# Four graph layers on one core: the weight products of three layers as seven half-size products

## The reference

```python
# L0: x1 = x @ W1 + b1 (512 wide); four times g = g + gcn(g), gate alpha = tanh(p[dst] + q[src] + gb) per edge
#     out = concat([x1, g])
# L1: two sage layers
h   = relu(x @ W_self0 + mean(x)[neighbours] @ W_neigh0 + b0)
out =      h @ W_self1 + mean(h)[neighbours] @ W_neigh1 + b1
# L2: attention
h = x @ W;  e = exp(-leaky_relu(al[src] + ar[dst], 0.1))
out = elu(segment_sum(e * h[dst], src) / (rowsum + 1e-5))
# L3: gcn with loops
out = relu(D^-1/2 (A + I) D^-1/2 (x @ W) + b)
```

## Time and profile before

| | |
|---|---|
| median of 3 runs | 1536.47 us (1536.3 to 1537.12) |
| profiled execution, span from the first to the last instruction | 1534.3 us |
| its own time outside the span | not shown |
| TensorE busy | 1515.2 us, 6985 matmuls |
| VectorE, ScalarE, GpSimd busy | 883.6, 753.9, 187.2 us |
| moved by DMA | 231.75 MB, mean 151 GB/s |
| granted TensorE clock | 0.998 |

### The profile page before, as it was taken

One profiled execution on the slowest core, in us unless ns is written; L12 is line 12 of the kernel. 1 busy time (PEld: TensorE's weight loads), 2 busy tenths in 40 slices (PEclk: granted clock), 3 DMA queues, 4 the chain that ended last, 5 costly groups with the idle time before them and its releaser, 6 DMA issues.

```text
span 1534.3 us, 19219 instructions
## 1 busy us (share of the span) xinstructions
PE 1515.2 (99%) x6985; PEld 1220.1 (80%) x6985; DVE 883.6 (58%) x1410; ACT 753.9 (49%) x1348; POOL 187.2 (12%) x307
## 2 busy tenths in 40 slices
PE   7999999999999999999999999999999999999997
PEld 6887877878887887788878777888888778877776
DVE  9888788887545442423332353567598356436346
ACT  7677767768633342433332233345696246533233
POOL 0110021333200000000000000212053013100003
PEclk9999999999999999999999999999999999999999
DMA  6333154226764424333354424554466248545336
GB/s 200 123 122 107 47 191 132 84 78 224 261 237 149 161 96 155 119 113 116 114 171 130 143 81 166 196 203 166 147 197 190 94 143 297 182 131 171 94 121 186
DMA packets 103198, 231.75 MB, mean 151 GB/s; under 512 B 23162, under 2 KB 25972, under 8 KB 103096
## 3 DMA queue, kind: packets, MB, share of 16 engines
q1 hardware_dynamic: 90126, 191.62, 39.3%
q10 hardware_dynamic: 12970, 38.77, 6.6%
HBM read 170.98 MB, written 59.37 MB: 150 GB/s over the span
## 4 chain that ended last, share of the span: by engine, by line
PE 96%; DVE 3%; ACT 1%; issue 0%; DMA 0%; POOLq 0%; DVEq 0%; ACTq 0%
PE bank L986 18%; PE bank L842 16%; PE bank L844 15%; PE bank L843 15%; PE bank L997 9%; PE bank L990 9%; PE bank L988 9%; PE bank L1075 2%; PE bank L912 2%; PE bank L880 1%; DVE oK L1801 0%; ACT Tt L1159 0%; DVE wl L1445 0%; DVE Tt L1483 0%; DVE oL L1791 0%
## 5 line engine op out<-in xcount | busy, mean ns | idle before, releaser
L842 PE MATMUL bank<-wh,xh 128*125 128x512 f32 x1032 | 413.4, 401 | 0.9 <-ACT xh L1124 0.9
L843 PE MATMUL bank<-wl,xh 128*125 128x512 f32 x1040 | 410.3, 395 | 0.0
L844 PE MATMUL bank<-wh,xl 128*125 128x512 f32 x1040 | 409.6, 394 | 0.0
L986 PE MATMUL bank<-Zh,Mh 125*125 125x512 f32 x990 | 394.9, 399 | 0.0
L1457 DVE TENSOR_TENSOR xl<-xs,xh 128x1000 fp32r<-128x1000 f32 x130 | 155.5, 1199 | 291.0 <-ACT xh L1124 290.6
L1124 ACT CAST xh<-xs 128x1000 fp32r<-128x1000 f32 x130 | 132.9, 1026 | 303.0 <-PE bank L844 290.8
L997 PE MATMUL bank<-Zl,Mh 125*125 125x512 f32 x590 | 232.5, 394 | 0.0
L844 PEld LDWEIGHTS bank<-wh,xl 128*125 128x125 f32 x1040 | 193.0, 186 | 48.9
L843 PEld LDWEIGHTS bank<-wl,xh 128*125 128x125 f32 x1040 | 193.1, 186 | 45.4
L842 PEld LDWEIGHTS bank<-wh,xh 128*125 128x125 f32 x1032 | 191.0, 185 | 46.6 <-ACT xh L1124 1.1
L986 PEld LDWEIGHTS bank<-Zh,Mh 125*125 125x125 f32 x990 | 183.5, 185 | 44.0
(11 more groups left out here) (188 smaller groups left out, 1825.3 us busy)
## 6 DMA issues: line engine op xcount, KB each, us to landing
xs<-xT_d SPq DMA_DIRECT2D x80, 500.0 KB, 3.6
Ar<-a_d SPq DMA_DIRECT2D x100, 312.5 KB, 3.4
xs<-hT_d SPq DMA_DIRECT2D x40, 500.0 KB, 3.4
x_d<-XO ACTq DMA_DIRECT2D x30, 512.0 KB, 4.7
R<-x_d SPq DMA_DIRECT2D x60, 256.0 KB, 4.2
xT_d<-XT ACTq DMA_DIRECT2D x30, 500.0 KB, 3.8
ws<-in_W SPq DMA_DIRECT2D x30, 256.0 KB, 3.6
Tt<-m_d SPq DMA_DIRECT2D x10, 625.0 KB, 4.5
```

The lines of the kernel that those rows point to most:

```text
L842: te.matmul(o, xh[i % 2][:, k, :], wh[s][:], start=(k == 0), stop=False)
L843: te.matmul(o, xh[i % 2][:, k, :], wl[s][:], start=False, stop=False)
L844: m = te.matmul(o, xl[i % 2][:, k, :], wh[s][:], start=False, stop=(k == 7))
L986: te.matmul(o, Mh[i][:, s, :], zh, start=(n == 0), stop=False)
```

## The change

```diff
+ORDER = (("sw", 0), ("sw", 1), ("ag", 0), ("sw", 2), ("sw", 3), ("ag", 1), ("sw", 4), ("ag", 2), ("sw", 5), ("ag", 3))
+    for kind, n in ORDER:
+        if kind == "sw":
+            jobs += [Job("sw", w=n, p=p, t=t) for p in range(NP) for t in range(NH)]
+        else:
+            jobs += [Job("ag", d, a=n, f=f) for d in range(NT) for f in (1, 0)]
...
+            def weight_product(j):
...
+                for k in range(4):
+                    q.wait_ge(s_sh, 4 * P + k + 1)
+                    q.wait_ge(s_sl, 4 * P + k + 1)
+                    a, b = uh[U_RING[u]][:, k * T:(k + 1) * T], ul[U_RING[u]][:, k * T:(k + 1) * T]
+                    te.matmul(o, a, SH[h][k][:], start=(new and k == 0), stop=False, skip_group_check=not new)
+                    te.matmul(o, a, SL[h][k][:], start=False, stop=False, skip_group_check=not new)
+                    m = te.matmul(o, b, SH[h][k][:], start=False, stop=(k == 3), skip_group_check=not new)
```

```diff
+    UNIT_AT.setdefault(max(_j - 3, _late - 1), []).append(_u)
+    UNIT_LOAD.setdefault(max(_j - 5, _late - 2), []).append(_u)
...
+            def load_unit(u):
...
+                if u >= 3:
+                    q.wait_ge(s_ul, u - 2)
...
+                sy.dma_start(us[U_RING[u]][:], src).then_inc(d_us[U_RING[u]], 16)
...
+            def unit_lower(u):
+                q.wait_ge(s_uh, u + 1)
+                ve.tensor_tensor(ul[U_RING[u]][:], us[U_RING[u]][:], uh[U_RING[u]][:].bitcast(f32), ALU.subtract).then_inc(s_ul, 1)
```

```diff
+            def weight_sums(m, which):
+
+                b = TB[m // 4 in (1, 2, 3, 4)]
+                q.wait_ge(d_tb, 32 * (m + 1))
+                for i in which:
+                    o, x, y = ((0, 1, 0), (1, 3, 1), (3, 3, 0), (2, 2, 3))[i]
+                    if i:
+                        q.wait_ge(s_tsum, 4 * m + i)
+                    po.tensor_tensor(b[:, o, :], b[:, x, :], b[:, y, :], ALU.subtract).then_inc(s_tsum, 1)
```

```diff
+            def node_sums(n):
...
+                q.wait_ge(s_te, TE[X_GROUP[I, NH + t]])
+                q.wait_ge(d_x1[S_X[n]], 16 * sum_uses(S_X, S_X[n], n))
...
+                chain("v", ve.tensor_tensor(o[:, QW:2 * QW], x5[:, 0:QW], x5[:, QW:2 * QW], ALU.add))
+                chain("v", ve.tensor_tensor(o[:, 0:QW], a[:, 0:QW], x5[:, 0:QW], ALU.subtract))
+                mine()
+                chain("v", ve.tensor_tensor(a[:, 0:QW], o[:, QW:2 * QW], a[:, 0:QW], ALU.subtract))
+                mine()
+                ve.tensor_tensor(a[:, QW:2 * QW], a[:, QW:2 * QW], a[:, 0:QW], ALU.subtract).then_inc(s_sum4, 1)
```

```diff
+            for j in range(NT - 1, NJ + 2):
...
+                    store_own(j - 1)
+                for n in S_STORE.get(j, []):
+                    store_s(n)
+                for m in SUM_STORE.get(j, []):
+                    store_sum(m)
+                for i in PAIR_LOAD.get(j, []):
+                    load_pair(i)
+                for u in UNIT_LOAD.get(j, []):
+                    load_unit(u)
```

More of the change, by code:

```diff
@@ L94, with micros, before @@
 NJ = len(JOBS)
[L97 to L133, removed]
 J0 = {k: next(j for j, job in enumerate(JOBS) if job.kind == "gate" and job.layer == k) for k in range(4)}
 LAST_GATE = J0[3] + NT - 1
+SJ = [[[next(j for j, o in enumerate(JOBS) if o.kind == "sw" and (o.w, o.p, o.t) == (w, p, t)) for t in range(NH)]
+       for p in range(NP)] for w in range(6)]
+AJ = [[[next(j for j, o in enumerate(JOBS) if o.kind == "ag" and (o.a, o.d, o.f) == (a, d, f)) for f in range(2)]
+       for d in range(NT)] for a in range(4)]
+YI = {j: i for i, j in enumerate(j for j, job in enumerate(JOBS) if job.kind == "ag")}
+def micros(job):
+    if job.kind == "x1":
+        return 5.6
+    if job.kind == "gate" or (job.kind == "ag" and job.a == 2):
+        return 6.95
+    return 2.78 if job.kind == "sw" else 4.63
+START = [0.0] + list(accumulate(micros(job) for job in JOBS))
+def before(j, us):
+    return max(k for k in range(j) if START[k + 1] <= START[j] - us)
 LAST_ORDER = (8, 9) + tuple(range(8))
@@ L280, in r_uses, with att_mul, tile_done @@
-def r_uses():
-    of, by, n = {}, {}, 0
-    for j, job in enumerate(JOBS):
-        many = (0, 2, 1, 1)[job.layer] if job.kind == "gate" else \
-            1 if (job.layer == 2 and job.second) or job.kind in ("att", "kept", "loop") or j in W2_AT else 0
-        of[j] = list(range(n, n + many))
-        for i in of[j]:
-            by[i] = j
-        n += many
-    return of, by
-R_OF, R_BY = r_uses()
+    return MCUM[j - NT]
+def att_mul(d):
+    return ECUM[-1] + d + 1
+def tile_done(a, d):
+    return MCUM[-1] + NT * a + d + 1
@@ new lines, in r_uses @@
+def r_uses():
+    uses, of = [], {}
+    for j, job in enumerate(JOBS):
+        if job.kind == "gate":
+            what = [("gate", j)] * (0, 2, 1, 1)[job.layer]
+        elif job.kind == "sw" and (job.p == 1 or (job.p == 4 and job.w in SELF)):
+            what = [("store" if job.w in SELF else "z", j)]
+        elif job.kind == "ag":
+            what = [("ag", j)] * (1 + (job.a == 1))
+        else:
+            what = []
+        of[j] = list(range(len(uses), len(uses) + len(what)))
+        uses += what
+    return uses, of
@@ L367, with bank_of @@
-WC_GROUPS = [i for j in range(NJ) for i, w, _ in GROUPS[j] if w == "wc"]
-STORE = {j: i for i, j in enumerate(STORES)}
+@dataclass
+class Group:
+    what: str
+    bank: int
+    d: int = 0
+    n: int = 0
+    job: int = 0
+def bank_of(j):
+    job = JOBS[j]
+    if job.kind == "x1":
+        return 4 + j % 2
+    if job.kind == "gate":
+        return (j - NT) % 6
+    if job.kind == "sw":
+        return 5 + job.t % 2 if job.p == 1 else (job.t + 1) % 5
+    return (5, 0, 1, 2, 3, 4)[YI[j] % 20 % 6]
@@ new lines, with row_group @@
+GROUPS, GROUPS_BEFORE, GROUPS_AFTER, PREV = places()
+TE = list(accumulate(g.what != "sum" for g in GROUPS))
+X_GROUP = {(g.job, g.d): i for i, g in enumerate(GROUPS) if g.what == "x" and g.n == 1}
+ATT_GROUP = {g.d: i for i, g in enumerate(GROUPS) if g.what == "att"}
+WC_LAST = max(i for i, g in enumerate(GROUPS) if g.what == "wc")
+def row_group(k, d):
+    if k:
+        return next(i for i, g in enumerate(GROUPS) if g.what == "row" and g.job == J0[k - 1] + row_pair(d).stop - 1)
+    return ROW_GROUP if d < 4 else next(i for i, g in enumerate(GROUPS) if g.what == "rows" and d in ROWS[g.n])
@@ L750, in late @@
                         store_left(d - 1)
-                elif job.kind == "gate" and job.layer == 2:
+                elif job.layer == 2:
                     if d == 0:
```

2295 lines of the change are left out of this document (1309 added, 986 removed).

## The result

The changed kernel takes 1559.93 us (median of 4 runs, 1558.33 to 1566.59) against 1536.8 (1536.3 to 1537.25) for the one before: ratio **1.0158** [1.0146, 1.017]. Forecast were 1465 us and a range of 1452 to 1490. It is slower, by 1.6%. The profiled execution took 1566.59 us; its span is 1564.8.

The account below looks back on a forecast made before the run. TensorE, almost never idle, was taken to bound the kernel: 1534.3 - 83.6 = 1450.7 us, plus charges of 1, 3, 5 and 3 gives 1462.7 of span, plus 2.2 gives 1464.9, forecast 1465 us; range 1452 to 1490.

Parts of the forecast that it names:

- The four charges: Added to the matmul floor of 1450.7 us: late handovers 1, weight sums 3, opening transfers 5, other bursts 3.
- TensorE's sum: Weight products: 360 fewer matmuls at 0.232 us each save 83.6 us, giving a floor of 1450.7 us.
- I charge 1 us (0 to 10): Weight products: jobs whose handover from VectorE or ScalarE is late cost TensorE 1 us, range 0 to 10.
- I take 3 us; ends 0 and 30: Gates and weight products: GpSimd's 96 weight sums stretch VectorE's operations, costing 3 us, range 0 to 30.
- one sum makes that 7.3, four jobs in a row 1.1 us late: Gate jobs: one weight sum lifts VectorE's 5.9 of 6.97 us per job to 7.3, unless it meets an idle moment.
- 89 of 97.6 us, still under: Weight products 0 to 3: sixteen sums each bring VectorE's load from 67.6 to 89 us of 97.6.
- 5 us there (0 to 15), and 3 for the other bursts: Transfer backlog and SyncE's queue at the first weight's opening cost 5 us; other bursts 3 (0 to 20).
- the ring's pace: Weight products: slow unit landings pace TensorE through three staging buffers; loss from 8.0 us, 1608 at 9; chance 0.04.
- GpSimd holds VectorE: Gates and products 1 and 3: weight sums make VectorE fall behind, +30 us, 1483 us; chance 0.1.
- more than 4% off TensorE: Sign that the sum is wrong: the chain that ended last shows more than 4% off TensorE.
- landing of 8 us: Sign that the sum is wrong: unit loads take over 8 us to land beyond the first product.
- VectorE's mean per split above 0.69 where sums run: Expected sign: VectorE's mean time to split a unit exceeds 0.69 us where GpSimd's weight sums run.

Follow-up runs that it names:

- v3: Changed kernel with unit loads first in SyncE's slots, plus each input's last node sum split over three slots: 1528.05 us, -15 against that order alone.
- e1: Changed kernel with GpSimd's weight sums on 16 columns instead of 512, transfers kept (results wrong): 1522.2 us, -38 us.
- e2: Changed kernel with thin weight sums and also their loads and stores thin, slabs loaded straight from the weights: 1523.51 us.
- f2: Changed kernel with 64 weight sums on VectorE, unit loads first, weight 0's sums waiting for products, row sums moved, last node sums split: 1503.14 us.
- e10: Changed kernel with SyncE's slots reordered: unit loads ahead of stores and pairs, last gate product's load one slot earlier: 1542.71 us, -17.
- v2: Changed kernel with unit loads first in SyncE's slots, plus attention's row sum behind the block's first half: 1530.75 us, -12 against that order alone.
- e5: Changed kernel with 64 of 96 weight sums (weights 1 to 4) on VectorE, their transfers in other slots: 1538.71 us, -21.
- u1: Kernel with all mends, but the 64 weight sums of weights 1 to 4 back on GpSimd: 1507.24 us against 1503.14, +4.
- e8: Kernel before the change with 15 pauses put into TensorE's program: 1581.9 us, +45.4 us for pauses of 34.8.

## Why the prediction was wrong

The four charges (1, 3, 5 and 3 us) add up to 12; measured were 82.8 us of new waits and 26.2 of half clock.

*TensorE's sum* (83.6 us, 0.232 per matmul) was right: the table's rest is 78 to 80 us lower.

*Handovers, "I charge 1 us (0 to 10)"* failed. The `DVE R` waits alone are 18.8 us. The argument went by mean load (69% of 97.6 us) and named the 2.8 us of four node sums, but charged nothing for what is queued behind them. In product 1 there are two banks for the sums in flight, so a combination that is one job late stops TensorE; all ten `DVE R` waits stand in a product 1. v3 priced the node sums' part: 15 us, with the clock.

*GpSimd, "I take 3 us; ends 0 and 30"*. The mechanism was right and the size wrong, by two steps. The line "one sum makes that 7.3, four jobs in a row 1.1 us late" took the diff's slots for times: GpSimd ran the first slab's four sums in 6.38 us within one job. And for the weight products "89 of 97.6 us, still under" was a mean over the stage again, while the sums come in pieces of 6 us over some two jobs; 30 us of the loss lie there. VectorE lost 53 us in all, and the kernel 38 by e1, 8 above my upper end. That end was also worked out wrong: a quarter of 116 x 1.35 us is 39, not 30.

*Transfers, "5 us there (0 to 15), and 3 for the other bursts"* went by bytes. 49 MB less gained nothing (e2, none of them at the opening), and a unit landed in some 5 us. (The page of the Trainium skill weighed there, "DMA: Bandwidth & Descriptors", Specifications, has about 358 GB/s for a core. Three slices of 37 us of f2 moved 377, 348 and 364, and 381 to 407 held for 30 us of its opening, so the rows keep the higher figure.) I wrote that SyncE's queue "now waits in it for stores of the node sums, with unit loads behind", and charged 5 us for that and the backlog of bytes together. The standing queue was the mechanism, and its order alone was worth 17 us (e10).

*Attention aggregation*: no term at all. The row transposes of a block now directly precede the next block's row sum on the same bank, eight waits, 9.9 us; v2 priced them at 12 with the clock.

*The clock*: no term at all, and the reading was at hand: "1.00 in the stretches that I looked at" holds because TensorE there never waited. 26.2 us.

The terms were also added as if they were independent. They are not: the same 64 sums on GpSimd instead of VectorE cost 21 us in the changed kernel (e5, with its other slots) and 4 with every other mend in (u1).

*Rivals*: the slower one, the ring's pace through landing times of 8 us and more, didn't happen (4.9 and 5.1 in the median). The loss came by another way, with the gain used up by several causes that I had put near zero, none of them over half of it. The rival "GpSimd holds VectorE" (+30 us) named the largest of them. Of the signs named, the chain's "more than 4% off TensorE" fired (40%), landing of 8 us didn't, "VectorE's mean per split above 0.69 where sums run" did (770 ns over all units). The waits of the first ten jobs were 18.8 us, slow matmuls included, not 3 to 8, and weights 4 and 5 were not free of them: they hold four of the ten `DVE R` waits, 9.1 us.

## What to carry to other kernels

When a change takes work from the engine that is never idle and gives it to three that are, price the order and not the load: for each new wait in a queue, what stands behind it, and for each slot, what really keeps an operation in it. Sum the waits at two prices: in e8 pauses of 34.8 us cost 45.4, nearly a third more, and in the changed kernel 82.8 us of new waits brought 26.2 of half clock. And where a change comes out slower, count the gain separately (the rest in the table): here it was whole, and a better order of loads and operations (f2) brought 57 us back.

## What was not expected of the hardware

TensorE's granted clock fell to 1.2 GHz behind single waits as short as 1.5 us (the ones before 1272.46 and 1340.88, each behind a group of row transposes) and came back after 3.4 or 6.8 us; six pauses of up to 1.70 us in the kernel before never did it, and of nine longer ones three had no effect. So no length of wait that is safe, or sure to slow the clock, comes out of these runs. A 128x512 subtraction on GpSimd takes 1.6 us beside VectorE and costs VectorE about 0.55 us (53 us for 96), nearly what the subtraction costs it when it does it itself (0.69).
